# The fourth attention pass of a graph network kernel takes in the stage that normalises its nodes

## The reference

```python
x = _layernorm(x + _L0_gnn_ref(...))   # two rounds of mean over neighbours
x = _layernorm(x + _L1_gnn_ref(...))   # weighted sum, two-layer MLP
x = _layernorm(x + _L2_gnn_ref(...))   # four terms of attention plus neighbour mean
x = _layernorm(x + _L3_gnn_ref(...))   # messages by edge, a gated update
```

```python
agg = segment_sum(msg, col); gcn = agg * deg_inv           # mean over the neighbours
kvs = einsum('lhm,lhd->hmd', ks, vs)                       # keys times values
num = einsum('nhm,hmd->nhd', qs, kvs) + vs.sum(0)          # queries times that
terms.append(BETA * gcn_i + num / den)
return (concatenate(terms) @ Wo_w + Wo_b) / H
```

## Time and profile before

| | us |
|---|---|
| median of 3 runs | 5326.28 (5324.18 to 5327.95) |
| span of the profiled execution | 5325.0 |
| fourth dense pass, first DVE instruction to last sum | 3862.45 to 4192.58 |
| stage of the nodes, first DMA to last | 4196.69 to 4275.18 |
| first gather of the message rounds | 4279.63 |

### The profile page before, as it was taken

How to read it: one execution, slowest core, us unless ns; L and a number is a source line. 1 busy time by engine, 2 the same in 40 slices (tenths; PEclk the granted TensorE clock), 3 DMA queues, 4 the chain that set the end, 5 groups by cost and what they waited for, 6 DMA issues and landing times. The chain is left out here.

```text
span 5325.0 us, 78049 instructions
## 1 busy us (share of the span) xinstructions
PE 4321.5 (81%) x26640; PEld 3018.0 (57%) x26640; DVE 2815.1 (53%) x7430; ACT 1451.2 (27%) x2914; POOL 3251.7 (61%) x3382
## 2 busy tenths in 40 slices
PE   4677866979868787788879997999889767777786
PEld 3444434545535556554446664666555467667775
DVE  6588886755367776535562315221432444455554
ACT  1377850010057664111120102010210122222222
POOL 2766626767767775075516661776177367777774
PEclk6789988989989999699989998999999898999998
DMA  4265559999933344195588887988697465555553
GB/s 145 45 61 80 91 100 194 199 182 187 202 80 101 104 126 109 60 289 159 168 265 271 270 248 250 280 268 253 228 303 241 130 171 144 143 149 146 151 153 82
DMA packets 1261118, 909.00 MB, mean 171 GB/s; under 512 B 446403, under 2 KB 1181934, under 8 KB 1260638
## 3 DMA queue, kind: packets, MB, share of 16 engines
q1 hardware_dynamic: 909866, 519.09, 39.3%
q0 software_dynamic: 102704, 232.38, 16.1%
q10 hardware_dynamic: 248132, 152.25, 9.9%
HBM read 696.10 MB, written 118.89 MB: 153 GB/s over the span
## 5 line engine op out<-in xcount | busy, mean ns | idle before, releaser
L1687 PE MATMUL ps<-adj_d,xs_d 128*128 128x464 bf16 (+1 forms) x4704 | 992.8, 367 | 60.1 <-DVE xs_d L1648 60.1
L3166 POOL DMA_INDIRECT rows_mg<-p_tab,src_idx x784 | 758.3, 967 | 273.4 <-issue 238.1
L1601 POOL DMA_INDIRECT rows_d<-xh_tab,src_idx x632 | 617.7, 977 | 479.8 <-POOLq L187 207.4
L1601 POOL DMA_INDIRECT rows_d<-x_tab,src_idx x512 | 499.1, 975 | 475.5 <-POOLq L187 264.4
L1687 PEld LDWEIGHTS ps<-adj_d,xs_d 128*128 128x128 bf16 x4704 | 466.1, 101 | 509.1 <-DVE xs_d L1648 61.9
L1295 POOL DMA_INDIRECT rows_d<-h_tab,slot_idx x490 | 497.0, 1014 | 266.9 <-issue 143.9
L2216 POOL DMA_INDIRECT rows_g<-x_tab,src_idx x444 | 434.2, 978 | 164.7 <-issue 127.3
L3263 PE MATMUL ps<-win_mg,turned_hot_mg 128*128 128x128 f32 x1568 | 341.2, 302 | 201.2 <-DVE pre_mg L3215 201.0
L1431 PE MATMUL ps<-adj_d,xs_d 128*128 128x512 bf16 (+1 forms) x2028 | 441.0, 375 | 54.6 <-DVE xs_d L1396 49.9
L1673 PEld LDWEIGHTS ps<-onehot_d,rows_d 128*128 128x128 f32 x3552 | 428.6, 192 | 66.6 <-DVE onehot_d L1619 33.5
L1673 PE MATMUL ps<-onehot_d,rows_d 128*128 128x72 f32 (+1 forms) x3552 | 421.4, 275 | 31.3 <-DVE onehot_d L1619 26.3
(11 more groups left out here) (442 smaller groups left out, 7541.4 us busy)
## 6 DMA issues: line engine op xcount, KB each, us to landing
adj_d<-adjacency SPq DMA_DIRECT2D x140, 812.0 KB
adj_d<-adjacency SPq DMA_DIRECT2D x84, 857.5 KB
attr_mg<-in_edge_attr SPq DMA_DIRECT2D x195, 256.0 KB
xp_g<-x_tab SPq DMA_DIRECT2D x70, 448.0 KB
k_rows_d<-k_tab ACTq DMA_DIRECT2D x56, 448.0 KB
loc_mg<-loc_rows SPq DMA_DIRECT2D x196, 128.0 KB
q_s<-q_tab SPq DMA_DIRECT2D x42, 448.0 KB
rden_s<-rden_tab SPq DMA_DIRECT2D x42, 448.0 KB
```

The source lines that it names most:

```text
L1601: nc.gpsimd.indirect_dma_start(rows[:, q % GR * K + k, :], None, table, bass.IndirectOffsetOnAxis(ap=src_idx[:, j:j + 1], axis=0)).then_in ...
L1687: last = nc.tensor.matmul(ps[:, m % 2, 0:w], xs[:, g * GW + k, e, :], adj[:, slot, k, 0:w], start=(g == 0 and k == 0 and e == 0), stop=(g ...
L3166: nc.gpsimd.indirect_dma_start(rows[:, q % RR, k, :], None, p_tab, bass.IndirectOffsetOnAxis(ap=src_idx[:, j:j + 1], axis=0)).then_inc(row ...
```

## The change

- `dense_pass` gets an argument `ending`. Its order of work is now a list of slots, each with pieces, groups, a tile or none, and for an ending an entered part. Without `ending` the list (`even_slots`) is the old order. With it (`ending_slots`, the fourth pass alone) pieces go two to a slot from slot 1 on; groups are placed by an estimate of their gathers' time, at most two to a slot; after the last piece the 14 parts of the node stage enter as soon as the blocks and the groups that their sums need are placed, at most every second slot while tiles run, and slots without a tile follow until the last part is through.
- `layer2_last` becomes the class `LastNodes` with the same steps, driven by the lists of entered parts (lags 0 to 6). It has one bank (4) for the turn while tiles run and banks 0 and 1 after them, one (5) for the turn back and one pair (6, 7) for the products. ACT issues its share loads and the stores of p and q rows.
- Its buffers take the place of those of the attention: `keys_values` holds K and value rows in one buffer, and `ending(spare)` starts again at the head of the spare plane. So all engines wait at the opening until all pieces are through (`begin`, `settle`).
- Before the first part changes x, x is copied to DRAM (`x_kept`, [P, NP] float32). `LastAgain`, the same steps again after a reload of x, stands in the fallback for graphs that need it, and is skipped here with it. The fallback of the fourth pass now stands after the node stage's work.
- The sums of a group with two heads lie in one bank (2 or 3) and not in two, and a group's matmuls run head by head. `key_sum` takes the place of two rows of biases. `value_parts` is longer. ACT waits for the last K/V piece before the next phase opens.

The core of the diff:

```diff
+NODE_PARTS = [(g * GC + half * BLOCK, GW - BW if half else BW) for g in range(G) for half in range(2)]
+TILE_US, GROUP_US, GATHER_US, PIECE_US, VISIT_US = 4.2, 1.75, 5.05, 1.6, 4.3
...
+                    def ending_slots():
+
+                        slots, visits, ready = [], [], [(c, nw * P) for c, nw in NODE_PARTS]
+                        clock, t, q, p, entered = 0.0, 0, 0, 0, -2
+                        while t < tiles or q < groups or ready or len(slots) <= entered + last_nodes.lag:
+                            took = pieces[p:p + 2] if t else []
+                            opens = p >= len(pieces)
+                            p += len(took)
+                            group = []
+                            while q < groups and len(group) < 2 and clock > 4.5 + GATHER_US * (q + 1):
+                                group.append(q)
+                                q += 1
+                            tile = t if t < tiles else None
+                            able = [v for v in ready if needs(*v)[1] <= q and (needs(*v)[0] < 0 or stored_at(needs(*v)[0]) < t or tile is None)]
+                            ask = None
+                            if opens and able and len(slots) - entered > (tile is not None):
+                                ask, entered = len(visits), len(slots)
+                                visits.append((*able[0], tile is None))
+                                ready.remove(able[0])
+                            if tile is None and not group and q < groups:
+                                group.append(q)
+                                q += 1
+                                clock = max(clock, 4.5 + GATHER_US * q)
+                            slots.append(Slot(took, group, tile, ask, None))
+                            clock += len(took) * 2.0 + len(group) * 0.9 + (4.4 if tile is not None else 2.0) + (3.2 if ask is not None else 0)
+                            t += tile is not None
+                        return slots, visits
...
+                    def final(eng, i):
+
+                        block, sums = needs(*visits[i][0:2])
+                        eng.wait_ge(cleared, 1)
+                        if block >= 0:
+                            eng.wait_ge(stored, block + 1)
+                        if sums:
+                            eng.wait_ge(added, sums)
...
                     def sums_of(q):
 
-                        bank = 2 + heads * (q % 2)
-                        return ps[:, bank:bank + heads, 0:NARROW]
+                        return ps[:, 2 + q % 2, :].rearrange("p (h n) -> p h n", h=heads)[:, :, 0:NARROW]
...
-                                for k in range(K):
-                                    for h in range(heads):
+                                for h in range(heads):
+                                    for k in range(K):
...
+            def begin(self, act, again=False):
+                if again:
+                    act.dma_start(xT[:, 0:NP], x_kept).then_inc(self.kept, 16)
+                else:
+                    act.dma_start(x_kept, xT[:, 0:NP]).then_inc(self.kept, 16)
+                for j in range(3):
+                    self.load(act, j)
...
+            def on_vector(self, line, ready):
+                dve = nc.vector
+                if line[0] is not None:
...
+                    dve.wait_ge(self.halved, j + 1)
+                    dve.wait_ge(self.kept, 16)
+                    nc.vector.tensor_tensor(x, x, a, ALU.add).then_inc(self.final, 1)
...
+            def on_tensor(self, line):
+                pe = nc.tensor
+                if line[3] is not None:
+                    j = line[3]
+                    c, nw, at = self.part(j)
+                    pe.wait_ge(self.normed, j + 1)
+                    if j:
+                        pe.wait_ge(self.in_place, j)
...
+                if line[4] is not None:
...
+                    pe.wait_ge(self.in_place, j + 1)
+                    if j:
+                        pe.wait_ge(self.q_made, j)
...
+                if line[0] is not None:
+                    j = line[0]
+                    c, nw, at = self.part(j)
+                    pe.wait_ge(self.final, j + 1)
+                    if self.before_turn(j) > 0:
+                        pe.wait_ge(self.normed, self.before_turn(j))
```

More of the change, by code:

```diff
@@ L1502, in dense_pass @@
                         opened.append(len(pieces))
-                        slots = max(work.parts for work in phase)
+                        most = max(work.parts for work in phase)
                         for g in range(G):
-                            for k in range(slots):
-                                pieces.append([(work, k, g) for work in phase if work.parts == slots] +
-                                              [(work, 0, g) for work in phase if work.parts < slots and k == slots // 2])
@@ L1508, in dense_pass @@
-                    for k, piece in enumerate(pieces):
-                        before = phases[opened.index(k) - 1] if k and k in opened else ()
-                        due[1 + k * (tiles - 1) // len(pieces)].append((before, piece))
-                    gathered = [[] for t in range(tiles + 1)]
-                    for q in range(groups):
-                        gathered[min(tiles, 2 + q * tiles // groups)].append(q)
-                    def beside(eng, t):
-                        for before, piece in due[t]:
+                            for k in range(most):
+                                pieces.append([(work, k, g) for work in phase if work.parts == most] +
+                                              [(work, 0, g) for work in phase if work.parts < most and k == most // 2])
@@ new lines, in dense_pass, with stored_at, needs @@
+                    pieces = [(phases[opened.index(k) - 1] if k and k in opened else (), piece) for k, piece in enumerate(pieces)]
+                    def stored_at(m):
+                        return order.index((m + 1, 2) if m else (1, G - 1)) if m < heads * blocks - 1 else tiles
+                    def needs(c, w):
+                        first_block = (heads - 1) * blocks
+                        covering = [first_block + b for b in range(blocks) if b * block_of < c + w]
+                        g = c // GC
+                        of_dense = c + w <= blocks * block_of
+                        sums = 0 if of_dense else groups if g == G - 1 else max(0, FINAL[g] - tail // K)
+                        return covering[-1] if c < blocks * block_of else -1, sums
@@ new lines, in even_slots @@
+                    def even_slots():
+                        slots = []
+                        for t in range(tiles + 1):
+                            slots.append(Slot([piece for k, piece in enumerate(pieces) if 1 + k * (tiles - 1) // len(pieces) == t],
+                                              [q for q in range(groups) if min(tiles, 2 + q * tiles // groups) == t], t if t < tiles else None, None, None))
+                        return slots
+                    def ending_slots():
[24 more added lines that the diff above has]
+                        return slots, visits
@@ new lines, in dense_pass, with beside @@
+                    if last_nodes:
+                        slots, visits = ending_slots()
+                        last_nodes.visit(visits)
+                        begins = min(k for k, slot in enumerate(slots) if slot.ask is not None)
+                    else:
+                        slots = even_slots()
+                    first_idle = min(k for k, slot in enumerate(slots) if slot.tile is None)
+                    def beside(eng, slot):
+                        for before, piece in slot.pieces:
@@ L1638, in add @@
                             nc.vector.tensor_tensor(a, a, sums_of(q), ALU.add).then_inc(added, 1)
-                        for t in range(tiles + 1):
-                            if t < tiles and splits_at(t) is not None:
-                                h, g = splits_at(t)
+                        for k, slot in enumerate(slots):
+                            if slot.tile is not None and splits_at(slot.tile) is not None:
+                                h, g = splits_at(slot.tile)
                                 s = h * G + g
```

420 lines of the change are left out of this document (245 added, 175 removed).

## The result

The changed kernel takes 5338.84 us (median of 18 runs) against 5325.35 us for the kernel before beside it: ratio 1.0031, 95% interval 1.0019 to 1.0043. It is slower by 0.3%, where 5322 us was forecast. Beside it again, in a later batch, it took 5350.95 us (median of 7) against 5323.39: 1.0042 (1.0028 to 1.0056). Two executions of later batches at a much lower clock (6681.04 us of the kernel without the copy, 7471.69 us of the kernel before) are left out of the comparisons.

A forecast was written before the change was run, and what follows sets the result against it. PE was taken to bound the fourth pass: 302.3 us of work plus the terms gave 412.4 us against 417.2, 4.8 less, of which 4 was kept: 5322 us. The 8-in-10 range was 5303 to 5340.

The forecast's parts named there:

- 1 start, slow clock: From the pass's first DVE instruction: 13.7 us to the first matmul, as now, and 3.4 us at half clock.
- 2 second K/V load: K/V 1 comes ahead of tile 1, so PE's wait for its load grows by the tile to 9.5 us.
- 3 K/V slots 2 to 7: At 309 GB/s a slot takes 11.45 us against PE's 9.7; the six slots together lose 9 us.
- 4 attention slots: Slots 8 to 17: each second piece waits 1.25 us for DVE to take the first one's bank; 12.5 us.
- 5 copy: After the last attention update: PE's first node turn waits about 5 us for the copy of x to land.
- 6 nodes beside tiles: In tile slots: 11 turns, 10 turns back and 9 products of the nodes add 23 us on PE.
- 7, 8 tail, boundary, pass: After the last tile: 27.5 us to the last row product, 4.5 to the next gather, 2.0 for the skipped general pass.
- the rest is small: Remaining edits (two-headed groups' order and bank, ACT's opening wait, row stores on ACT's queue, longer skipped body): each 0.
- A (the engines give way): Fourth pass: K/V and copy waits fall to 5, 0 and 0, the tail to 25: 5302 us; chance 0.22.
- B (ACT's queue starved): K/V slots 2 to 7: ACT's queue keeps 131 GB/s, a slot takes 15.7 us: 5349 us; chance 0.08.
- C (the clock): Slots 1 to 18: gaps hold the clock low; a tenth of 190 us gives 5332, a third 5352; chance 0.07.
- D: Node visits beside tiles: each of the 11 holds PE 2 us, 22 more: 5344 us; chance 0.09.

The follow-up runs named there:

- the small edits: Changed kernel with the fourth pass in its old order and the old node stage behind it, against before: 6073.64 us, 1.0014; again 5337.53 us, 1.0031.
- the pieces apart: Changed kernel with the second piece of each slot entered behind the slot's groups, against the kernel before: 6058.06 us, 0.9989.

## Why the prediction was wrong

The section was forecast at 412.4 us and took 426.6. By its own terms, measured in the trace of after:

| term | forecast | measured |
|---|---|---|
| 1 start, slow clock | 13.7, 3.4 | 13.6, 8.5 |
| 2 second K/V load | 9.5 | 10.9 |
| 3 K/V slots 2 to 7 | 9 | 12.7 |
| 4 attention slots | 12.5 | 16.2 |
| 5 copy | 5 | 4.8 |
| 6 nodes beside tiles | 23 | 21.0 |
| 7, 8 tail, boundary, pass | 34.0 | 36.6 |

The work of 302.3 us is in both; the measured terms then sum to 426.6. Slot 2 has one group and not two, so the six K/V slots hold 54.4 us of PE's work of the 67.1 they last. The last tile ends 390.0 us after the start (forecast 378.4). That 5338.84 us lies inside the forecast's range, 1 us from its end, is owed to the width of the range: the forecast was faster and the kernel is slower.

**The step that failed is "the rest is small".** The paragraph went through instructions, queues and waits and put the small edits at 0. It did not ask where the buffers would lie. On the chip of 5323 us these edits alone measured 1.0031 (1.0019 to 1.0044), some 16.5 us, against 1.0042 (1.0028 to 1.0056) for the whole change: three quarters of the loss by the ratios, half of it by the medians (14.1 of 27.6 us), and the intervals allow from a third to all. So it failed beside the terms of the section, which account for the other part.

What of this is shown and what is argued: that moving the buffers, and nothing else, takes 5 to 6% of what the DMA engines move per busy time in the K/V phase of the first pass is shown by the three runs of the moved buffers (271 or 272 against 286 and 287 GB/s per share). That this makes the 16.5 us is argued. For it: where the engines are the bound a rate lower by 6% is time, and the K/V phases of the first and fourth pass, with a share of 1.1, stand in the two stages that grew most, by 9.6 and 6.0 us. On the chips of 6023 to 6064 us PE is behind and the share in the first pass's K/V phase is 0.88 to 0.95, so the slower transfers may be mostly hidden, and the shift alone measured 0.01 to 0.15%. Against it: a share above 1 is not enough. In the first layers, too, the engines move less per unit of share with the moved buffers (194 / 1.08 = 180 and 194 / 1.12 = 173), and PE is busy nine tenths of these 600 us. Before, then the small edits:

```profile
840.00:1440.00 600.00, 537.87 (x3143) 324.30 (x3141) 367.82 (x773) 43.06 (x76) 446.54 (x446) 0.96 1.08 194
```

```profile
840.00:1440.00 600.00, 540.92 (x3138) 322.33 (x3137) 366.64 (x776) 44.08 (x77) 443.14 (x445) 0.96 1.12 194
```

Nothing is lost there: the profile of the small edits is 9.8 us longer than that of before, made of 9.3 less up to the third layer, 9.6, -0.6 and 4.1 in the first three passes, 6.0 in the section and 0.1 in the message rounds. The third pass grew without any change of its rate, and the 9.6 us of the first pass are no more than the two profiles of before differ by (10.7). Last, neither the 960 bytes alone nor the small edits at the old places were timed on a chip of 5325 us. So the 16.5 us are not pinned to the shift: that the small edits cost is shown, why they do is open.

**Terms 2 and 3** rest on transfers of before, term 2 on when the second load landed and term 3 on the rate of the earlier trace rows. The changed kernel doesn't have that rate: 279 GB/s, not 309. With it, a slot of 2.943 MB takes 2.943 / (0.279 - 0.052) = 13.0 us by the forecast's own formula. The slots took 67.1 / 6 = 11.2 us, so the forecast of 11.45 was near by luck, with two errors against each other: the engines were slower, and part of what the six slots need had been loaded before them (an estimate: at 279 GB/s 67.1 us move 18.7 MB, and six slots with their gathers want 6 x 2.943 + 67.1 x 0.052 = 21.1). The sum also left out the half microsecond between the pieces of a K/V slot that the same line states, six times 0.5 = 3.0 us.

**Term 4** is the largest loss inside the moved stage. Its mechanism was right: nine waits of 1.2 to 1.4 us for DVE at L270 between two pieces and one of 2.1 put down to a load. They were foreseen as a cost of the new order. On the slower chips, where these waits are 21.5 to 27.3 us long, setting the second piece behind the groups is worth 16 us in one batch, and 10 and 26 in two others (with the copy in parts). The size, 16.2 instead of 12.5, is 13.8 us of waits plus some 0.2 of start behind each.

**The slow clock** was taken from the first tile and one K/V piece only. In after it also follows the wait of 10.8 us into tile 1 (5.56 us from start to start instead of 4.35) and the wait of 4.8 us: the groups and the tile behind the first turn lost 3.8 us. Term 5 was right in size (4.8). Its worth is open: with the pieces apart, the copy in parts is not measurably faster than the copy in one, and the kernel without the copy has no like to be held against.

**Rivals.** A (the engines give way) fell: in the K/V slots they stayed full. B (ACT's queue starved) fell: the six K/V slots took 11.2 us each, where it needed 15.7 and decided from 13.2. C (the clock) has a small part of the truth: 0.95, 1.00 and 0.97 in the three stretches, and 5 us more than forecast in all. D fell clearly: 11 visits beside tiles cost 21.0 us, near the 20.4 of their work, with 148.3 of 154 us busy. What ended slower was none of the four: each looked in the section alone, and by the middle values half of the loss or more came with edits that none of them had in view.

**What is left of the idea.** Without the handovers the kernel is 0.1% faster than before on chips of 6023 to 6064 us, with an interval that touches or comes near 1. The forecast of -5 us for the section set the old stage of 85 us against what comes back (23 us of PE work, 34 of tail and boundary, and the waits): a small difference of large terms, which 14 us turn round (5.1 of clock, 3.7 each in terms 3 and 4, 2.6 in the tail, 1.4 in term 2, less 2.3 in the others).

**Two smaller readings.** The forecast's chances of faster and slower come from its own parts to 0.26 and 0.225, not 0.27 and 0.21; nothing hangs on it. And the earlier trace rows bear out turns by packet in direction only: ACT's queue has 25349 packets to SP's 12561 in one and 568 to 850 in the other, not one to one. One to one would need both queues to have work all the time, which the rows don't tell.

## What to carry to other kernels

An edit that changes the size of any shared buffer moves all that are declared behind it, and in some stages the DMA engines then move less per busy time: print the addresses of both kernels before calling an edit free, and where a kernel is measured to 0.2%, pad so that they stay. Two pieces that wait for the same bank should not stand side by side in an engine's order: a tile or two groups between them hide most of the handover of 1.3 us. And time the small edits as a kernel of their own: here they make, by the middle values, half of the loss or more, and the forecast had them at nothing.

## What the runs showed of the hardware

The amount that the DMA engines move per busy time can depend on where in a partition the destination lies: 286 to 290 GB/s per unit of share against 269 to 274 in the first pass, with all buffers 960 bytes lower. The first lay at a distance of 0 (gathered rows) and 128 bytes (K/V rows, `raw`, tiles) from a multiple of 256, the second at 64 and 192. In the second and third pass, where the gathered rows move from 160 to 224 and the K/V rows from 32 to 96 (`raw` and tiles as in the first), it does not change: 299 and 300 in the two rows of the second pass, 300 and 299 in the same profiles' third.

The Trainium skill, "DMA: Bandwidth & Descriptors", How a descriptor splits into AXI transactions, says that a descriptor that doesn't begin at a multiple of 256 bytes has a first transaction from the boundary below, whose unused bytes cost beats of 32 bytes all the same; it says so of reads. An estimate by that page: a packet of 512 bytes would cost 16, 18, 20 or 22 beats at a distance of 0, 64, 128 or 192, a tile's row of 980 bytes 35.6 and 35.3 on the average of its seven places. Of a slot of the old order (7 tile rows, 14 K/V rows, 3.5 of `raw`, 3.5 gathered) it makes 655 beats before and 695 after, 6% more, and the trace agrees in the sum for the first pass. It doesn't agree by queue: in the pair of rows above a packet of SP's queue takes 6% longer, where the estimate has the tiles unchanged, and one of POOL's no longer, where it has the gathers grow most, by an eighth. Nor does it agree in the second and third pass, where by the same rule a K/V row grows from 17 to 19 beats and a row of `raw` from 20 to 22. No run here moves one buffer alone, so which of them costs, and why, stays open.
